# A graph network in one program: layer 3's second MLP product of two row tiles put ahead of the first product of the other two, and one-hots and bias rows made while the keys load

## The reference, cut to what matters

```python
# layer 3, after its attention (a is 512 x 512)
o = a @ Wo
x = _layernorm(h + o, ln1_g, ln1_b)
f = jax.nn.relu(x @ W1 + b1) @ W2 + b2      # W1: 512 x 256, W2: 256 x 512
return _layernorm(x + f, ln2_g, ln2_b)
...
x = _layernorm(x + layer3(x), axis=-1)      # the result
```

## Time and profile before

| what | value |
|---|---|
| time, median of 3 runs | 552.86 us (551.17 to 553.95) |
| the profiled execution: its own time, its span | 554.51 us, 552.7 us |
| PE busy | 515.1 us, 93% |
| DVE busy | 391.3 us, 71% |
| ACT, POOL busy | 230.0 us (42%), 266.2 us (48%) |
| mean granted TensorE clock | 0.989 |
| the edge weights' matrix: load issued, first used | 144.55 us, 167.73 us (6.9 us to landing) |

### The profile page before, as it was taken

The page is one execution under the profiler, slowest core; times in us unless marked ns, Lnnn a source line. Parts: engine busy times, 40 slices in busy tenths (PEclk is TensorE's granted clock), DMA queues, the critical chain, the costliest instruction groups (busy, mean ns, idle before and its releaser), DMA issues.

```text
span 552.7 us, 7901 instructions
## 1 busy us (share of the span) xinstructions
PE 515.1 (93%) x2540; PEld 352.5 (64%) x2540; DVE 391.3 (71%) x969; ACT 230.0 (42%) x479; POOL 266.2 (48%) x258
## 2 busy tenths in 40 slices
PE   7899999999998999998999999998999999899981
PEld 3344444446775565876788888878887786564770
DVE  6799969999977786876676754656327625775567
ACT  2102450006406775566442142234634225785446
POOL 5377777767346775004342651343342653867000
PEclk9999999999999999999999999999999998999996
DMA  6921400000465220424553553222453753100001
GB/s 200 371 99 46 114 1 1 0 0 2 153 208 173 62 73 1 115 66 138 188 161 84 183 168 99 76 76 58 118 189 78 246 172 85 49 2 1 0 2 76
DMA packets 30170, 54.39 MB, mean 98 GB/s; under 512 B 4962, under 2 KB 6446, under 8 KB 29624
## 3 DMA queue, kind: packets, MB, share of 16 engines
q1 hardware_dynamic: 17212, 29.50, 17.0%
q0 software_dynamic: 11696, 18.91, 11.8%
q10 hardware_dynamic: 1228, 5.54, 2.6%
HBM read 51.78 MB, written 2.17 MB: 98 GB/s over the span
## 4 chain that ended last, share of the span: by engine, by line
PE 67%; DVE 17%; ACT 7%; issue 3%; DMA 3%; POOL 1%; SPq 1%; DVEq 0%; POOLq 0%; ACTq 0%
PE bank L535 15%; PE bank L512 9%; PE bank L514 9%; PE bank L513 9%; PE bank L641 5%; PE bank L628 3%; PE bank L719 3%; PE bank L721 3%; PE bank L720 3%; PE bank L619 2%; DMA keyb<-edge_keys 2%; ACT sp L863 2%; DVE h L1145 2%; DVE h L1144 1%; DVE eq L1174 1%
## 5 line engine op out<-in xcount | busy, mean ns | idle before, releaser
L371 POOL TENSOR_TENSOR wl<-wraw,wh 128x512 fp32r<-128x512 f32 (+1 forms) x78 | 103.9, 1348 | 92.5 <-DMA wh<-w 15.5
L535 PE MATMUL bank<-hot 128*128 128x512 bf16 x528 | 114.6, 379 | 5.0 <-DVE hot L1193 5.0
L535 PEld LDWEIGHTS bank<-hot 128*128 128x128 bf16 x528 | 51.4, 98 | 68.2 <-DVE hot L1193 7.1
L415 POOL DMA_INDIRECT edge_bias<-ewn,cell_at x68 | 74.9, 1102 | 37.7 <-issue 16.6
L512 PE MATMUL bank<-wh,tl 128*128 128x512 f32 x176 | 69.5, 395 | 1.3 <-DVE ql L1327 0.8
L514 PE MATMUL bank<-wh,th 128*128 128x512 f32 x176 | 68.8, 391 | 0.0
L513 PE MATMUL bank<-wl,th 128*128 128x512 f32 x176 | 68.7, 391 | 0.0
L1193 DVE TENSOR_SCALAR hot<-iota,pair_dst,digit 128x1024 bf16<-128x1024 f16 x68 | 49.1, 723 | 0.0
L863 ACT ACTIVATE sp<-sp,peak 128x512 f32<-128x512 f32 x44 | 31.8, 723 | 24.5 <-DVE peak L1365 24.3
L1174 DVE SCALAR_TENSOR_TENSOR eq<-keyb,key,later 128x384 f16<-128x384 f16 (+1 forms) x68 | 40.0, 609 | 0.0
L512 PEld LDWEIGHTS bank<-wh,tl 128*128 128x128 f32 x176 | 33.1, 188 | 9.9 <-issue 3.4
(11 more groups left out here) (213 smaller groups left out, 1064.2 us busy)
## 6 DMA issues: line engine op xcount, KB each, us to landing
wraw<-w SPq DMA_DIRECT2D x26, 256.0 KB
wh<-w POOLq DMA_DIRECT2D x6, 1024.0 KB, 5.8
keyb<-edge_keys ACTq DMA_DIRECT2D x4, 1088.0 KB, 9.9
wh<-w_rel POOLq DMA_DIRECT2D x4, 1024.0 KB, 5.8
wraw<-w_rel SPq DMA_DIRECT2D x16, 256.0 KB
wraw<-w_qkv SPq DMA_DIRECT2D x8, 256.0 KB
wh<-w_o POOLq DMA_DIRECT2D x2, 1024.0 KB, 5.8
wraw<-w_o SPq DMA_DIRECT2D x8, 256.0 KB
```

Of the source, the lines that this page charges most:

```text
L371: pool.tensor_tensor(wl[n % WSLOTS][:, k, 0:width], wraw[:, q % 3, 0:width], wh[n % WSLOTS][:, k, 0:width], ALU.subtract).then_inc(s["w_lo ...
L415: pool.indirect_dma_start(out=bias_dram, out_offset=bass.IndirectOffsetOnAxis(ap=cell_at[:, c:c + 1], axis=0), in_=ewn[:, c:c + 1], in_off ...
L535: mm = pe.matmul(ps(name)[:], hot[:, slot, 0, i * P:(i + 1) * P], hot[:, slot, 1 + kind, :], start=False, stop=last, skip_group_check=True)
```

## The change

In the PE program, W2's product (`f3`) of tiles 0 and 1 is put between the two halves of `hid3`, and the turns move: turn 1 into the middle of tile 3's `o3` product, turns 2 and 3 behind part 0. ACT and DVE take the halves in the new order. At the start, DVE builds the third block of one-hots before it waits for the keys, with the masks, `second`, the bias rows and `ident_r` between its chunks, and marks the first block on its own; the loop begins one block later. In the counts, `new_rest(b + 1)` goes ahead of `both_sums(b)`.

```diff
@@ PE @@
             for i in range(T):
+                def second_turn(k):
+                    mixed(3, i)(k) if i == 0 else None
+                    if i == 3 and k == 3:
+                        turn(4, h, 7, 1)
                 begin(("o3", i))
-                finish(product(("o3", i), t_tile(i), w_tile(18), ready=mixed(3, i)), ("o3", i))
-                if i >= 2:
-                    turn(4, h, 7, i - 2)
+                finish(product(("o3", i), t_tile(i), w_tile(18), ready=second_turn), ("o3", i))
+                if i == 2:
+                    turn(4, h, 7, 0)
             w_ready(19)
+            pe.wait_ge(s["add2_ready"], 4)
             for part in range(2):
...
-                    if part == 0:
-                        turn(4, h, 7, 2 + f)
-            w_ready(20)
-            pe.wait_ge(s["add2_ready"], 4)
-            for i in range(T):
-                name, cut = ("f3", i), slice(i * P, (i + 1) * P)
-                bias(name, 0)
...
+                if part == 0:
+                    turn(4, h, 7, 2)
+                    turn(4, h, 7, 3)
+                    w_ready(20)
+                for i in (2 * part, 2 * part + 1):
+                    name, tile = ("f3", i), slice(i * P, (i + 1) * P)
+                    bias(name, 0)
...
@@ ACT @@
+            half_hidden(0, 0)
+            half_hidden(0, 1)
             turned(4, 2)
-            half_hidden(0, 0)
             turned(4, 3)
-            half_hidden(0, 1)
+            deviation(8, 0, h[:, 0, :])
+            deviation(8, 1, h[:, 1, :])
             half_hidden(1, 0)
             half_hidden(1, 1)
...
+            deviation(9, 0, h[:, 0, :])
+            deviation(8, 2, h[:, 2, :])
+            normalise(9, 0)
+            deviation(9, 1, h[:, 1, :])
+            deviation(8, 3, h[:, 3, :])
+            normalise(9, 1)
+            deviation(9, 2, h[:, 2, :])
+            deviation(9, 3, h[:, 3, :])
@@ DVE, start @@
+            for slot in range(RING):
+                dve.wait_ge(s["hot_used1"], FIRST_PLACED * RING + slot - RING + 1)
+                build_chunk(FIRST_PLACED * RING + slot, slot)
+                if slot == 1:
+                    build_masks()
...
+                if slot == 2:
+                    dve.wait_ge(s["ld_bias"], 64)
+                    bias_rows(rows[:], slice(0, P), 0)
+            link(dve.tensor_copy(ident_r[:], ident[:]))
             dve.wait_ge(s["ld_later"], 16)
             dve.wait_ge(ld_keys[0], 16)
             dve.wait_ge(ld_keys[1], 16)
-            with dve.Fori(FIRST_PLACED, CBLOCKS[0]) as b:
+            for half in range(2):
+                mark(0, 2 * half)
+                mark(0, 2 * half + 1)
+                settle(0, 0, half)
+            with dve.Fori(FIRST_PLACED + 1, CBLOCKS[0]) as b:
@@ DVE, counts @@
             new_rest(4)
-            both_sums(4)
...
-            for b in (6, 7):
+            for b in (5, 6, 7):
                 new_rest(b)
-                both_sums(b)
-            link(dve.tensor_copy(ident_r[:], ident[:]))
+                both_sums(b - 1)
+            both_sums(7)
@@ DVE, end @@
+            half_low(0, 0)
+            half_low(0, 1)
             turned(4, 2)
-            half_low(0, 0)
             turned(4, 3)
-            half_low(0, 1)
-            half_low(1, 0)
-            half_low(1, 1)
...
             centre(8, 0, ("f3", 0), h[:, 0, :])
             centre(8, 1, ("f3", 1), h[:, 1, :])
             affine_and_add(8, 0, 0)
...
+            half_low(1, 0)
+            half_low(1, 1)
+            affine_and_add(8, 1, 0)
+            centre(8, 2, ("f3", 2), h[:, 2, :])
+            shift_of(9, 0)
+            centre(8, 3, ("f3", 3), h[:, 3, :])
+            affine_and_add(8, 2, 0)
+            shift_of(9, 1)
+            affine_and_add(8, 3, 0)
```

More of the change, by code:

```diff
@@ L811, in _ @@
                     finish(mm, name)
[L812 to L820 removed]
+                if part == 0:
[5 more added lines that the diff above has]
+                    bias(name, 0)
+                    finish(product(name, lambda k: (hidh[:, k, tile], hidl[:, k, tile]), w_tile(20), 2, start=False,
+                                   ready=(lambda k: pe.wait_ge(s["hidl_ready"], 8 + i + k + 1)) if i % 2 == 0 else None), name)
         @block.scalar
@@ L1309, in _ @@
             new_rest(4)
-            both_sums(4)
-            build_masks()
-            dve.wait_ge(s["ld_ident"], 16)
-            link(dve.tensor_reduce(second[:], ident[:, 1::32], AX_X, ALU.add))
-            link(dve.tensor_scalar(second[:], second[:], -1.0, None, ALU.mult))
-            new_rest(5)
-            both_sums(5)
-            dve.wait_ge(s["ld_bias"], 64)
-            bias_rows(rows[:], slice(0, P), 0)
-            for b in (6, 7):
+            for b in (5, 6, 7):
                 new_rest(b)
-                both_sums(b)
-            link(dve.tensor_copy(ident_r[:], ident[:]))
+                both_sums(b - 1)
+            both_sums(7)
             def part_low(name, f, dst, top, add, highs, done):
@@ L1643, in _ @@
             affine_and_add(8, 0, 0)
-            for i in range(1, T):
-                if i + 1 < T:
-                    centre(8, i + 1, ("f3", i + 1), h[:, i + 1, :])
-                affine_and_add(8, i, 0)
-                if i < T - 1:
-                    shift_of(9, i - 1)
+            half_low(1, 0)
[7 more added lines that the diff above has]
+            affine_and_add(8, 3, 0)
             for i in (T - 2, T - 1):
```

12 lines of the change are left out of this document (3 added, 9 removed).

## The result

| kernel | median us | lowest to highest, runs |
|---|---|---|
| before | 551.80 | 551.17 to 553.95, 8 |
| changed | 549.26 | 547.49 to 550.58, 8 |

The ratio is 0.9942, 95% interval [0.9925, 0.9959]: 3.2 us faster (2.3 to 4.1). Forecast were 548.5 us (546.8 to 550.9) and a gain of 4.4 us. The 548.5 was reckoned from 552.86, the median of three runs; the eight runs give 551.80, so the two numbers for the time lie nearer to each other than the two gains. The profiled execution of the changed kernel took 547.83 us, 6.7 less than the 554.51 of the one before. That is more than the runs differ by, so I split the 6.7 by stage.

What follows compares the result with a forecast made beforehand. It took PE (67% of the chain) to bound the kernel, with gains where PE waits or DVE and ACT run alone. 0.3 + 2.4 + 1.7 = 4.4 us off the median gave 548.5 us, range 546.8 to 550.9.

Steps and rivals of the forecast that it cites:

- The third block, 0.3: At the start, the third block built while the keys load: of PE's 2.57 us wait all but 0.3 us returns later.
- its other outcome, worth 1.1: At the start, POOL doesn't hold DVE's first chunk, saving 0.8 us: this part gives 1.1 us in place of 0.3.
- The counts, 2.4: From `q0` to `v0`, 3.5 us of DVE work leave and banks come free before PE asks: 2.4 us saved.
- the bound of 2.7: Upper bound of the counts' gain: the 24.58 us from `q0` to `v0` less 96 steps of 0.228.
- The two idle times: PE's waits in the counts, 1.11 us ahead of `k0`'s second product and 0.85 for `ql`, both counted as saved.
- The end, 1.7: At the end, tiles 0 and 1 are finished while tiles 2 and 3 are still in PE: 1.7 us saved.
- the slower case: The clock falls ahead of part 0 and stays down to part 1's end: 10 us on top, 558.5; slower, chance 0.05.
- The short fall: At the end, the granted clock falls only as briefly as in attention 3 (3.4 us): costs 1.7, 550.2 in all.
- The end gains nothing: Rival: part 1 starts 1.7 us late, waiting for turned tiles 2 and 3; 2.7 in all, 550.2; chance 0.12.
- The bias rows land late: Rival at the start: bias rows land behind the keys, 0 to 1.7 gained, about 552; chance of nothing 0.07.
- DVE's idle time is of one execution alone: Rival: DVE's 4.73 us idle at 79.62 is the profiled execution's alone; counts give 1.1, 3.1 in all, 549.8; chance 0.22.
- my 2.7: Start and counts together as reckoned, 0.3 + 2.4 = 2.7 us faster than the kernel before.

Runs made afterwards that it cites:

- front_only: The kernel before with the changes of the start and of the counts alone, the end as before: 552.65 us, ratio 0.9973 to the kernel before.
- order_only: The kernel before with `new_rest(b + 1)` ahead of `both_sums(b)` from bank 4 on and nothing else: 554.72 us, ratio 1.0017.
- tl_first: The changed kernel with DVE's low part of tile 1 (`tl`) ahead of `centre(7, 3)`: 548.97 us, ratio 0.9899 to the kernel before.
- best: The changed kernel with `tl` of tile 1 ahead of `centre(7, 3)` and the start's side work behind blocks 4 and 5: 548.98 us, 0.9893 of the kernel before.
- peeled: The changed kernel with the third block built right away and the start's side work behind blocks 4 and 5: 551.65 us, ratio 0.9934 to the kernel before.

## Why the prediction came out as it did

**The third block, 0.3: near, and partly by luck.** No bias row was waited for, the loop began at 29.07 (28.9), the 13th chunk at 29.99 (30.1). Two errors cancel in this. POOL held the first of the chunk's two instructions, not the second, so the chunk was done at 20.99 where 20.49 was reckoned (the tie went to POOL; its other outcome, worth 1.1, did not come); masks and `second` took 1.8 us (21.64 to 23.46) in place of 2.38. The wait ahead of the 13th chunk was 0.56 in place of 2.2, as PE itself came late at half clock; since DVE gave it that chunk at 29.99 either way, the slow matmuls cost nothing here. What the working did not see is that DVE is busy without a pause from 35 to 67 us and so sets the length of the first sweep: taking the side work out brings 1.9 us there, and costs them in the second. The 3.73 us in which it stood idle for the keys were the free room, and the side work filled them. The stretch between the sweeps took 2.7 in place of 2.2, which ate the 0.3: 0.05 remain.

**The counts, 2.4: right in the traces, a little small.** Measured 2.61, inside the bound of 2.7, and `v0` comes 21.9 to 22.0 us behind `q0` in all ten profiles that have both the new order and the side work out of the counts, 24.2 to 24.6 in the four others. The timed runs of `front_only` don't confirm the size (1.5 for start and counts together). The two idle times were added up as if each were a price of its own. `order_only` shows that they are not: ending the first alone gives nothing, as `ql` sets the end of the stretch.

**The end, 1.7: right as a mechanism.** 1.9 in the profile without a fall. Part 0 starts 521.50 - 494.99 = 26.5 behind the mark, before 26.1: 0.4 lost, reckoned 0.45. From the first `f3` to the last step it takes 543.10 - 525.23 = 17.9, as forecast. Taken from part 0 (521.50, reckoned 526.28, 4.8 apart), `centre(8, 2)` at 534.76 was reckoned at 534.9 and the last step at 543.10 at 543.2. Not foreseen was a wait of 0.33 for `hidl` behind part 1. (Among the signs the prediction gives 14.6 and 15.5 us for the same stretch of before; rows 9 and 10 give 15.5.) The timed gain of the end alone, 0.6 (-0.4 to 1.7), leaves its size open.

**What was priced too low** is one clause: that PE's idle time ahead of part 0, "2.0 us in place of 1.6" (1.78 measured), costs only what it delays. It was put among the slower case, at a chance of 0.05, with the argument that "1.60 and 1.45 us of waiting did not bring it down before". The short fall was priced at 1.7 and costs 1.5; it comes in three of six profiles with that wait, though in neither of the two of the changed kernel itself. If it comes in half of the executions, it costs 0.75 (an estimate), and with the 0.3 of the start that would be most of the 1.2 between the reckoned 4.4 and the measured 3.2 (2.3 to 4.1). This is argued: no run shows how often the changed kernel has the fall, and the rival below makes up the 1.2 as well. The second timing gave 0.9929, or 3.9 us.

**The rivals.** The end gains nothing: fell as worked out (part 1 waits for nothing), though in the profiles with a fall it nearly comes to the same (52.6 against 53.0). The bias rows land late: fell. DVE's idle time is of one execution alone: the idle time stands in 8 of 14 profiles, in all four with the old start and in two of five with the new one, so its premise fell for profiled executions. Its number (3.1 gained) lies nearer to the measured 3.2 than mine, and `front_only`, where no fall behind part 0 was profiled, gained 1.5 (0.2 to 2.7), next to its 1.4 and far from my 2.7. No profile shows the old order without the idle time, and timed executions show no DVE. It stays open whether the gain of the counts is smaller there.

## What to carry to other kernels

Before filling an engine's wait, ask which engine sets the length of the whole stretch. Here PE's wait of 2.57 us looked like the gain, but DVE set the length, and its own idle time was the room in which other work cost nothing. Before moving work into a later stretch, count what that stretch has free. Of several waits in a row on one engine price only the last one that is released by the same other engine, and test it with the order alone. And when an edit lengthens a wait of PE just ahead of dense matmuls, try the producer that ends it first: here one swapped line went with 1.0 to 2.7 us in the medians of three pairs, more than the 0.3 of the earlier start itself, though why is not settled. The lowest ratios found are those of `tl_first` and `best`, 0.9899 and 0.9893 of the kernel before; their intervals overlap with that of the changed kernel in the same group.

## What the runs showed of the hardware

TensorE's granted clock fell to 0.50 for 3.4 us, 0.0 to 0.8 us behind the restart of PE after a wait of 1.78 us, in three of six profiles; in none of three after 0.91 us, none of four after 1.60 us, and not in the one after 2.50 us. The first 7 to 10 one-hot matmuls took 0.43 us each in seven of 14 profiles and 0.22 in six. Where DVE set the length of the stretch the half clock cost nothing (60.2 us in both `peeled` and `best`); where DVE had less to do, the profile with the late clock took 59.5 and the one without 58.4.

DVE waited for PE's release of a slot for 2.3 to 4.9 us near 78 to 82 us in 8 of 14 profiles, while PE's records show it working. In the other six no wait there was above 1.5 us. Right behind it PE itself waits for DVE in six of the eight, 0.4 to 1.2 us. In the profiled pair it went with 1.7 us more in the second sweep (63.70 and 61.98), but `tl_first`, without it, took 63.3 as well, so the 1.7 can't be put down to it. What delays these releases, and whether it occurs without the profiler, no run here tells.
